# Fetching the rows of every 64th gathered tile by 128 single-row DMAs from SP instead of one indirect DMA from GpSimd

## The reference

```python
h = relu(layernorm(x))                                   # 12500 x 64
edge_in = concat([h[src], h[dst], dist], axis=1)         # 212500 x 129
e = silu(edge_in @ eW1 + eb1)                            # 212500 x 128
e = silu(e @ eW2 + eb2)
agg = segment_sum(e, src, 12500)                         # 12500 x 128
out = x + silu(concat([h, agg], axis=1) @ nW1 + nb1) @ nW2 + nb2
```

## Time and profile before

| | us |
|---|---|
| median of 3 runs | 3712.42 |
| lowest and highest | 3707.98, 3724.45 |
| the profiled execution: its own time | 3720.55 |
| its span, first to last instruction | 3718.7 |

### The profile page before, as it was taken

One profiled execution on the slowest core, in us unless ns is written; L12 is line 12 of the kernel. 1 busy time (PEld: TensorE's weight loads), 2 busy tenths in 40 slices (PEclk: granted clock), 3 DMA queues, 4 the chain that ended last, 5 costly groups with the idle time before them and its releaser, 6 DMA issues.

```text
span 3718.7 us, 78198 instructions
## 1 busy us (share of the span) xinstructions
PE 2677.6 (72%) x21722; PEld 2217.4 (60%) x22026; DVE 2035.6 (55%) x7353; ACT 1578.0 (42%) x3444; POOL 2115.2 (57%) x2181
## 2 busy tenths in 40 slices
PE   7888787875667776767766667767777667776668
PEld 3544454543566666666666666666666666666667
DVE  8777777775444444444444444444444444444444
ACT  4666566663333333333333333333333333333333
POOL 0355545555666666666666666666666666666660
PEclk8999999997898889998889998898888999898889
DMA  2011111111222222222222222222222222222213
GB/s 77 22 24 29 19 29 25 23 26 25 48 48 47 48 48 48 47 48 49 48 47 49 48 48 47 48 48 48 47 48 48 48 49 47 48 48 45 44 43 141
DMA packets 366686, 168.84 MB, mean 45 GB/s; under 512 B 290486, under 2 KB 336110, under 8 KB 366574
## 3 DMA queue, kind: packets, MB, share of 16 engines
q0 software_dynamic: 72992, 121.26, 13.0%
q1 hardware_dynamic: 271390, 35.69, 6.2%
q10 hardware_dynamic: 22192, 10.53, 1.0%
HBM read 138.64 MB, written 28.67 MB: 45 GB/s over the span
## 4 chain that ended last, share of the span: by engine, by line
PE 65%; issue 25%; ACT 4%; another core or an unknown queue 3%; DVE 3%; DMA 0%; POOL 0%; ACTq 0%; DVEq 0%; SPq 0%; POOLq 0%
PE bk L1211 13%; PE bk L1220 12%; PE bk L1201 10%; PE bk L1199 7%; PE bk L1189 4%; PE bk L1063 3%; PE bk L1209 2%; PE bk L1097 2%; PE bk L1129 1%; PE bk L1051 1%; PE bk L1052 1%; ACT BIG L1339 1%; PE bk L1231 1%; PE bk L1278 1%
## 5 line engine op out<-in xcount | busy, mean ns | idle before, releaser
L535 POOL DMA_INDIRECT GA<-q_d,IX x1760 | 1682.4, 956 | 1038.5 <-remote 504.0
L911 DVE TENSOR_TENSOR BIG<-bk,BIG 128x128 f32 x1760 | 512.3, 291 | 1374.6 <-PE bk L1220 684.3
L1211 PE MATMUL bk<-W,ED 128*128 128x128 f32 x3520 | 541.2, 305 | 476.1 <-issue 466.5
L1427 ACT ACTIVATE ED<-bk,eb1c 128x512 f32<-128x512 f32 x440 | 302.3, 687 | 1326.5 <-remote 1110.7
L1201 PE MATMUL bk<-OHS,P 128*128 128x128 bf16 x5280 | 641.2, 244 | 0.0
L1199 PE MATMUL bk<-identf,GA 128*128 128x128 f32 x1760 | 559.5, 318 | 79.8 <-issue 65.3
L500 POOL DMA_INDIRECT rec_d<-BIG,GA x312 | 336.7, 1079 | 409.4 <-issue 296.9
L1201 PEld LDWEIGHTS bk<-OHS,P 128*128 x5280 | 530.7, 112 | 56.5
L1211 PEld LDWEIGHTS bk<-W,ED 128*128 128x128 f32 x3520 | 541.9, 220 | 16.9
L1220 PE MATMUL bk<-ED 128*128 128x128 f32 x3520 | 526.7, 295 | 0.7 <-ACT ED L1432 0.7
L902 DVE SCALAR_TENSOR_TENSOR GA<-c_bc,EW,GA 128x128 f32<-128x128 f32 x1760 | 498.7, 344 | 9.9 <-DMA GA<-q_d,IX 9.9
(11 more groups left out here) (243 smaller groups left out, 3051.0 us busy)
## 6 DMA issues: line engine op xcount, KB each, us to landing
GA<-q_d,IX POOLq DMA_INDIRECT x1760
q_d<-QS SPq DMA_DIRECT2D x14, 448.0 KB
u_d<-QS ACTq DMA_DIRECT2D x98, 64.0 KB
P<-u_d SPq DMA_DIRECT2D x8, 768.0 KB, 11.5
rec_d<-BIG,GA POOLq DMA_INDIRECT x312
rec_d<-ED SPq DMA_DIRECT2D x16, 220.0 KB, 10.1
RW<-rec_d SPq DMA_DIRECT2D x110, 32.0 KB
HT<-hT_d ACTq DMA_DIRECT2D x99, 32.0 KB
```

The costliest lines, as they stand in the source:

```text
L535: e.indirect_dma_start(G[k % 4 * U + u], None, q_d, bass.IndirectOffsetOnAxis(ap=IX[g // BG % 2][:, k * U + u:k * U + u + 1], axis=0))\
L911: e.tensor_tensor(AGG[:, ds(v, P)], banks[6 + k % 2][:, u * P:(u + 1) * P], AGG[:, ds(v, P)], ALU.add).then_inc(s["ad"], 1)
L1211: last = e.matmul(z[:, u * HF:(u + 1) * HF], E1[k % 2][:, u * P:(u + 1) * P], W2[:, :], start=False, stop=(u == U - 1))
L1427: e.activation(E1[k % 2], banks[2 + k % 2][:, :], ACT.Silu, bias=eb1c[:, :]).then_inc(s["e1"], 1)
```

## The change

Of every 16 groups, one tile (the last tile of group 27, 43, 59, ..., 427: NSPEC = 26 tiles in all) is no longer gathered by GpSimd. SP fetches its 128 rows by 128 DMAs of one row of 512 bytes each. For that:

- Before the loop SP loads the records of these 26 tiles (`RAWS`, 26 partitions of 2 KB), and DVE extracts the row numbers (`ROWI`) and raises `ri`.
- SP loads 4 row numbers at a time into registers, and issues four DMAs, each with its register as address. They go into two buffers of their own (`GS`), and count up four semaphores (`s_row`). 32 rows are issued, then one `load_rec`, and so on, so SP's order of work is 128 rows and four `load_rec` for every 16 groups. Before the rows of special tile sp it waits until DVE has weighed special tile sp - 2. SP's loop is gone: it is written out.
- In `weigh`, DVE reads a special tile from `GS` and writes the result to `G`, where PE reads it as before. It waits for two row semaphores, and for `z1` to reach n - 3.
- DVE's loop body grows from 8 groups to 32 (13 iterations), with 16 groups ahead of it and 8 behind.

```diff
+SG = 16
+SFIRST, SLOT = 16 + 11, 15
+NSPEC = (NG - 8 - SG) // SG
...
+        GS = [sb(f"GS{k}", [P, HF], fp32) for k in range(2)]
+        RAWS = LATE[32:32 + NSPEC, 0:4 * P]
+        ROWI = LATE[32:32 + NSPEC, 4 * P:5 * P]
...
+        def special(g, slot):
+            return slot == SLOT and g >= SFIRST and (g - SFIRST) % SG == 0 and (g - SFIRST) // SG < NSPEC
+        def landed(g, slot):
+            return 16 * sum(not special(h, slot) for h in range(slot // U, g + 1, 4))
...
-            with e.Fori(1, NG // (2 * BG)) as i:
-                for k in range(2):
-                    load_rec(i, k)
+            r0 = (SFIRST % SG * U + SLOT % U) * P
+            e.dma_start(RAWS.bitcast(fp32), rows_d[0:(NSPEC + 1) * SG * U * P, :].rearrange("(s r) w -> s r w", r=SG * U * P)
+                        [1:NSPEC + 1, r0:r0 + P, :].rearrange("s r w -> s (r w)")).then_inc(s["rs"], 16)
+            def rows(sp, a, b):
+                if a == 0:
+                    ge(e, s["st"], SFIRST + (sp - 2) * SG + 1 if sp >= 2 else 0)
+                for r in range(a, b, 4):
+                    vs = nc.values_load_multi_w_load_instructions(
+                        ROWI[sp:sp + 1, r:r + 4], engines=[mybir.EngineType.SP], min_val=0, max_val=NPAD - 1,
+                        skip_runtime_bounds_check_because="destinations are rows of q_d")[1]
+                    for j, v in enumerate(vs):
+                        e.dma_start(GS[sp % 2][r + j:r + j + 1, :], q_d[ds(v, 1), :]).then_inc(s_row[sp % 2][j % 2], 16)
+            e.wait_ge(s["ri"], 1)
+            e.wait_ge(s_hq[0], 32 * (NCH // 2))
+            e.wait_ge(s_hq[1], 32 * (NCH // 2) + 16)
+            nb = 2
+            for sp in range(NSPEC):
+                for part_ in range(SG // BG):
+                    rows(sp, part_ * P * BG // SG, (part_ + 1) * P * BG // SG)
+                    load_rec(nb // 2, nb % 2)
+                    nb += 1
+            while nb < NG // BG:
+                load_rec(nb // 2, nb % 2)
+                nb += 1
...
+                    if special(g, k * U + u):
+                        continue
                     e.indirect_dma_start(G[k % 4 * U + u], None, q_d,
...
-            def weigh(i, k):
-                ew = EW[k // BG][:, :].bitcast(fp32)
+            def weigh(n, i=None):
+                ew = EW[n // BG % 2][:, :].bitcast(fp32)
                 for u in range(U):
-                    w = k % BG * U + u
-                    e.wait_ge(s_g[k % 4 * U + u], i * 32 + (k // 4 * 16 + 16))
-                    ins = e.scalar_tensor_tensor(out=G[k % 4 * U + u], in0=c_bc[:, :], scalar=ew[:, w:w + 1],
-                                                 in1=G[k % 4 * U + u], op0=ALU.mult, op1=ALU.add)
+                    w = n % BG * U + u
+                    slot = n % 4 * U + u
+                    own = G[slot]
+                    if special(n, slot):
+                        sp = (n - SFIRST) // SG
+                        own = GS[sp % 2][:, :]
+                        for q in range(2):
+                            e.wait_ge(s_row[sp % 2][q], i * (8 * P) + 8 * P)
+                        e.wait_ge(s["z1"], i * BODY + (n - 3))
+                    else:
+                        e.wait_ge(s_g[slot], landed(n, slot) if i is None
+                                  else i * (landed(n + BODY, slot) - landed(n, slot)) + landed(n, slot))
+                    ins = e.scalar_tensor_tensor(out=G[slot], in0=c_bc[:, :], scalar=ew[:, w:w + 1], in1=own,
+                                                 op0=ALU.mult, op1=ALU.add)
...
+            BODY = 2 * SG
             decode(0, 0, 0)
             decode(1, 1, 0)
             build(0, 0, 0)
-            for k in range(8):
...
-            with e.Fori(1, NG // 8 - 1) as i:
-                for k in range(8):
...
+            e.wait_ge(s["rs"], 16)
+            e.tensor_scalar(ROWI, RAWS.rearrange("s (r w) -> s r w", w=4)[:, :, 1], 13, MARK - 1,
+                            ALU.logical_shift_right, ALU.bitwise_and).then_inc(s["ri"], 1)
+            for n in range(SG):
+                run(n)
+            with e.Fori(0, (NG - 8 - SG) // BODY) as i:
+                for n in range(SG, SG + BODY):
+                    run(n, i)
+            for n in range(NG - 8, NG):
+                run(n)
```

More of the change, by code:

```diff
@@ L268, in gnn @@
         names = ("hl um uc us fa es sp bt pk oq sm cs rr hc fb cst io w ms ed edc o1 f1 cc lb tl tb df dq m mb o2 p2 tt lbb bi cm vw cb tr tc dc da co vp xs x8 xt sl bv a1 so mm dd dr up rec ai sd0 sd1 sd2 sd3 acc ix "
-                 "xm sq h t1 ht pq p1 r1 r2 p2c p3 rcp ep dk qc fin htd qd ini scat0 scat1 scat2 scat3 "
+                 "xm sq h t1 ht pq p1 r1 r2 p2c p3 rcp ep dk rs ri qc fin htd qd ini scat0 scat1 scat2 scat3 "
                  "oh st ad tp z1 z2 ap oT of e1 e2 zero var rt hd fz fu fo fd outs one").split()
@@ L274, in gnn @@
         s_rec = [sem(f"s_rec{k}") for k in range(2)]
+        s_row = [[sem(f"s_row{k}{j}") for j in range(2)] for k in range(2)]
         s_g = [sem(f"s_g{k}") for k in range(4 * U)]
@@ L912, in add, with run @@
                                     AGG[:, ds(v, P)], ALU.add).then_inc(s["ad"], 1)
+            def run(n, i=None):
+                g, b = (n, 0) if i is None else (i * BODY + n, i * (BODY // BG))
+                m = n + 1
+                if m < NG:
+                    build(g + 1, m % 8, b + m // BG if m % BG == 0 else None)
+                weigh(n, i)
+                if n >= 2:
+                    add(g - 2, (n - 2) % 4)
+                if m % BG == 0 and n + 5 < NG:
+                    decode(b + m // BG + 1, (m // BG + 1) % 2, (m // BG + 1) // 2 if i is None else i * (BODY // 8) + (m // BG + 1) // 2,
+                           g + 1)
+            BODY = 2 * SG
             decode(0, 0, 0)
@@ L916, in _ @@
             build(0, 0, 0)
-            for k in range(8):
-                build(k + 1, (k + 1) % 8, (k + 1) // BG if (k + 1) % BG == 0 else None)
-                weigh(0, k)
-                if k >= 2:
-                    add(k - 2, k % 4)
-                if k % BG == BG - 1:
-                    decode(2 + k // BG, k // BG, 1, k + 1)
-            with e.Fori(1, NG // 8 - 1) as i:
-                for k in range(8):
-                    build(i * 8 + (k + 1), (k + 1) % 8, i * 2 + (k + 1) // BG if (k + 1) % BG == 0 else None)
-                    weigh(i, k)
-                    add(i * 8 + (k - 2), k % 4)
-                    if k % BG == BG - 1:
-                        decode(i * 2 + (2 + k // BG), k // BG, i + 1, i * 8 + (k + 1))
-            for g in range(NG - 8, NG):
-                if g + 1 < NG:
-                    build(g + 1, (g + 1) % 8, (g + 1) // BG if (g + 1) % BG == 0 else None)
-                weigh(g // 8, g % 8)
-                add(g - 2, (g - 2) % 4)
+            e.wait_ge(s["rs"], 16)
[8 more added lines that the diff above has]
+                run(n)
             for g in (NG - 2, NG - 1):
```

## The result

The changed kernel took 3985.2 us in the median of four runs, against 3714.8 us for the kernel before in the same runs: 1.073 times as long, with an interval of 1.070 to 1.0757. The profiled execution has a span of 3980.4 us. Forecast were 3684 us. The time is 270 us longer, and it sits in the main loop.

The account below looks back on a forecast made before the run. It took POOL's cycle of four gathers per group, with z1 following the last one, as the bound. -32.5 (gathers) + 3 (stretching) + 1 (start) = -28.5 us gave 3684 us from 3712.4; 8-in-10 range 3675 to 3732.

Parts of the forecast that it names:

- SP's 3328 row DMAs: SP's queue in the main loop: 0.62 us a row against a limit of 0.75, so no cost while SP keeps up.
- SP becomes the bound: Rival, chance 0.12: a row costs over 0.75 us, load_rec and rows come late, DVE waits; near 4027 us at 0.85.
- three parts: SP's price of a row: 0.25 us issue, 0.16 us registers and gaps, 0.21 us load of row numbers.
- POOL's term: Gathers in the main loop: z1 comes when POOL's four gathers finish, so one less in 26 groups saves 32.5 us.
- A gather less: 26 groups of the main loop: three gathers instead of four, 1.25 us shorter each, -32.5 us.
- The cycle: Main-loop group: 0.24 us to the first gather, three steps of 1.25, 0.94 last gather, 1.2 behind it, 6.13 us.
- The gathers stretched: Row DMAs lengthen main-loop gathers: +3 us taken, at most 66; as a rival 3746 us, chance 0.10.
- The code fetch: DVE's longer loop body: fetching at 13 branches hidden by slack, cost nothing; unhidden 38 us, 3718 us in all.
- No gain: Rival on the main loop: gather count doesn't make the 6.17 us period, or longer gathers cancel it; 3705-3720 us, chance 0.22 (with code fetch).

Follow-up runs that it names:

- fixed addresses: Changed kernel, its 3328 row DMAs at addresses fixed in the program, no row numbers loaded: 1.0033 of the kernel before on slower chips, 0.992 on a quicker one.
- memset run: Kernel before plus a 0.55 us memset on GpSimd ahead of each third gather: 3642.4 us against 3641.1.
- half of the rows: Changed kernel with SP fetching 64 of each special tile's 128 rows: 1.0037 of the kernel before, on another chip 1.0026.
- every 32 groups: Changed kernel with 13 special tiles instead of 26, rows spread over 32 groups: 1.0088 of the kernel before on slower chips, 0.9962 on a quicker one.
- long body alone: Changed kernel with no special tile: GpSimd gathers all tiles, DVE's 32-group body stays; 3643.1 us against 3640.8 for the kernel before, 1.0006.
- kernel without rows: Changed kernel without SP's row DMAs and DVE's waits for them, 26 tiles weighed from old rows: 3605.1 us against 3640.8 for the kernel before, 0.9906.
- records first: Changed kernel with each load_rec issued ahead of its 32 rows: 1.0776 of the kernel before on slower chips, 0.9915 on a quicker one.

## Why the prediction was wrong, point by point

**The step that failed** is the term "SP's 3328 row DMAs", taken at 0.62 us a row with 0.75 as the limit, and with it the sentence that they "cost nothing as long as SP keeps up". Measured are 0.856 us a row, 0.59 with the same instructions and no gathers, and 0.33 to 0.37 with fixed addresses. The sentence is wrong by itself too: where SP keeps up, the rows still cost some 50 us. The rival "SP becomes the bound", given 0.12, is what happened, and in the way that it was told: `load_rec` late, decode waiting 546 us, SP never idle. Its price, with 0.85 us a row, was 343 us over the forecast, 4027 us; measured were 3985. The range, up to 3732 us, left this rival out.

**Why the price was too low.** Each of the three parts was read from a row that can't show a pause. The issue of 0.25 us was read at the start of the program, with no gather running. ACT's 0.16 us of registers was read just behind silu1, at 2003.35, and the load's bound of 0.21 us from DVE's add, just behind silu1 too, the moment in the group when z1 has just got through. At that moment no pause shows, in the changed kernel either: ACT's moves are 29 ns in all 88 cases, beside SP's of up to 1400 ns. Here are ACT's in the changed kernel, from 1000 to 3400 us:

```profile
L1491 ACTq MOVE HT<-hT_d x88: 29/29/29, 1000.5 to 3393.1; - x88
L1491 ACTq DMA_DIRECT2D HT<-hT_d x88: 482/482/483, 1000.5 to 3393.1; - x88
```

SP's rows, however, run through the whole group. A clue was in the trace of before: PE's product ended at 2011.69 and its semaphore came 3 us later, while gathers ran. I read it as a lag of one semaphore and used it for POOL's term, and never asked what else it might hold back. The held semaphores and SP's pauses come together on the slower chips, and neither shows on the quicker ones. In the changed kernel's trace they also come at the same moments. From 1500 to 3400 us 457 updates of `z1` and `tp` were over 0.7 us late, and 434 of them would have come, without the delay, inside a pause of SP. Of the 89 that came at once one would have, while SP is in a pause for half of the time. That makes one cause likely; what it is isn't shown.

**A gather less, -32.5 us:** right in size, 34 us measured (0.9906), and in that the group follows the number of gathers. The cycle that it was worked out from, with 1.2 us fixed behind the last gather, is refuted by the memset run, and a single group was 4.70 us against the 4.92 forecast. So that the size came out is in part luck.

**The gathers stretched, +3 us:** the duration didn't grow at all (950 ns). But there is a cost beside it that had no term: some 0.013 of the time (near 50 us) with half of the rows, with fixed addresses and with every 32 groups, though SP isn't the bound in any of them and DVE waits for none of its DMAs. It is more than the change can gain, so on these chips the forecast would have failed even with a row below 0.75 us. It sits behind the last gather of each group, in a still later `z1`. By what it comes there isn't shown.

**The code fetch, nothing:** right, 1.0006 (0.9992 to 1.0019) for the long body alone. By the Trainium skill's rule (Runtime: NRT & Kernel Launch, Instruction fetch mechanics) each of the 13 far branches forces a fetch. The profiles' pages do list more fetched instructions, 161 packets with the long body alone against 59 before (246 in the changed kernel, whose SP also has the rows written out), but the run gives them no price. That they lie in DVE's slack is argued, not shown.

**"No gain":** its point, that the period isn't made by the count of gathers, is refuted by the kernel without rows. The sentence of the Trainium skill that stood beside it (DMA: Bandwidth & Descriptors, Issuing engines are not separate DMA queues) says that a second issuer saves only the sequencer's time. Here the second sequencer's time was exactly what ran out.

**In sum:** -34 us for the gathers, and SP's pace: 26 x (109.6 - 97.6) = +312 us, makes +278; measured are +270 us. The 109.6 are read from the slow loop itself, so this says where the time is lost and is no second proof of why. On the quicker chips records first measured 27 us less and fixed addresses 23 less, near the forecast's 28.5. There the number fits by another way than the forecast's: no tail of 1.2 us stands behind the gathers, and GpSimd's four steps make the group.

**Open** stays what pauses SP and holds z1, whether it is GpSimd's issuing or the gathers' transfers, and whether it hangs on the gather's size. The memset run excludes a fixed tail behind the last gather. Open is also whether the profiler's recording has a part in it. All runs here have spans and clocks, so all were recorded, and on the slower chips records of semaphore updates are missing from the trace while gathers run. No version with row DMAs was found that beats the kernel before on the slower chips, while records first beats it on a quicker one.

## What to carry to other kernels

Work that is moved to an idle queue costs that queue's rate, and the rate must be read from rows that run at the same moments as the moved work will: a median or a row from a quiet moment hides pauses of 0.7 us on instructions of 29 ns. Look at the longest duration beside the median, and keep a margin: a queue at 0.62 of 0.75 us has none, and past the limit the loss is the whole loop's, here 312 us against a gain of 32.5. Ask how many instructions each moved DMA needs (here a load for four rows, and a register operation, a move and the DMA for each), because fixed addresses at one instruction a row were free of the bound. Don't take two equal rates as proof of which one sets the pace: look at which side waits. And where a semaphore comes microseconds behind the instruction that raises it, ask what else on the chip may be held up with it.

## What the runs showed of the hardware

- While GpSimd gathers, on the slower chips, SP's instructions are held for some 0.7 us and more at a time (longest record of a move 1400 ns), and the updates of PE's semaphores come some 3 us behind their product, most of them while SP is paused too. With the gathers left out, on a chip of the slower kind, every move took 29 ns and `z1` 0.24 us.
- Chips differ by 20% for the same kernel, 3641 to 3715 us and 3079 us. Most of it goes with this lag: 6.1 to 6.2 us a group against 4.97, which is four gathers. Some 100 us lie ahead of the loop (silu1 first starts at 887 us in the long body's run, at 794 us in records first).
- A DMA of one row at an address from a register costs SP 0.56 us where nothing pauses it (a load of four numbers is 0.56 us, 0.14 a row), one at a fixed address 0.33 to 0.37 us.
- A gather of 64 rows takes GpSimd 920 ns, one of 128 rows 955.
- 1664 or 3328 single-row DMAs beside the gathers cost about 0.013 of the time on the slower chips, even where no one waits for their issue. The time is lost behind the last gather of each group.
